# First layer of a two-layer cross-attention kernel: scores three heads ahead, values split once for all heads, two low parts on GpSimd

## Chip, cores and metric

The kernel runs on one core of one Trainium2 chip. The metric is the device time of one execution in microseconds (us). Shorter is better. The core's engines run side by side and meet only at semaphores: TensorE (PE in the rows, its weight loads PEld), VectorE (DVE), ScalarE (ACT), GpSimd (POOL), and SyncE (SP), which here only issues DMAs.

## What is computed

Two cross-attention layers, one after the other, over 4 batches of 512 queries, 512 context rows, 320 channels in 20 heads of 16. The part that the change touches is the first layer:

```
q = x @ Wq.T                      # 20 heads of 16
text = context[:77]; ip = context[77:]
out_text = softmax(q k_text.T / 4) @ v_text
out_ip   = softmax(q k_ip.T   / 4) @ v_ip      # a softmax of its own
x = (out_text + out_ip) @ Wo.T + bo + x
```

The second layer has the same sizes (508 text rows, 4 image rows, one more product) and uses another step function, which the change leaves alone.

## The kernel before

**Precision.** Products run in TensorE's rounded 32-bit format. To keep accuracy a number is split in two: a *high* part (rounded) and a *low* part (the number minus its high part), and the products of the parts are added up.

**Batch.** For each of the four batches the program does: 20 heads of layer 0, some dense products (k1, output projection, q1, the Gram matrix, v1), 20 heads of layer 1, then the inputs of layer 0 for the next batch (k0, q0, v0t, v0i) woven into the closing arithmetic of layer 1, then the output projection (tr1, y). The first three batches are turns of a loop, the fourth is written out.

**Heads of layer 0.** Every engine has a function `step0` of its own, called once per head by `run_heads` (two lead-in steps, a loop of four turns of four heads, four heads written out). In step n (head n is the one whose values are used):

- TensorE computes the scores of head n+2, queries by rows, in two halves (`scores_half`, `ps_s`), from which only the row maxima are wanted; the scores of head n+1 transposed, keys by rows, in four blocks (`scoresT_of`, `ps_t`, two buffers); the product values times probabilities of head n (`values_high`, `values_low`, `ps_w`, eight matmuls, four on high parts and four on low parts); a transpose of the maxima of head n+2 (`head_maxT`, `ps_m`); and the transposes back of the result (`ps_b`).
- ScalarE takes each transposed block twice, as exp rounded (`probsT_high`, line 454) and as exp in full (`probsT`, line 462); `shift` (line 447) copies the maxima into `q_slot`, so that the next transposed scores come out shifted; line 471 copies the head's result `ps_w` to SBUF (shown as `probs`, a buffer that is reused).
- VectorE takes the maxima (lines 638, 639), forms the low part of blocks 0, 1 and 2 (`lowT`, line 628), and adds up the result (line 653, `out_all`).
- GpSimd forms the low part of block 3 (line 376) and, for each head, copies the values of head n+2 from `v0_sb` into `v0_slot` as high parts (line 364, two CASTs) and subtracts to get the low parts (line 370, two subtractions). Both tiles are called `v_sb` and `v_slot` in the rows. These copies wait for `oT_moved`, the copy of line 471, since they overwrite the slot of the head just used.
- SyncE loads q and k parts of a head into one of four slots when the head four before it is done (`load_slots`).

The order on each engine is the order in which the code is written; nothing is reordered. `probsT` has one buffer, `probsT_high` and `probsT_low` have two each.

**Between the batches.** `v0_text` and `v0_ip` (ScalarE, lines 506 and 512) copy the value projections of the next batch from the ring of four PSUM banks into `v0_sb` and free the banks. VectorE runs a serial chain at the same time (lines 768 to 813; the last multiplications are line 805, the last addition, line 813, releases `heads_ready`). TensorE's stream there is v0t, v0i 0 to 3, then the transposes tr1 (line 1069), which wait for `heads_ready`, then y. Job i of the ring needs the bank of job i-4 to be freed.

Of the kernel before, what the change touches and what calls it, by code (L numbers as in the profile page):

```python
# [5 lines left out]
ACT = mybir.ActivationFunctionType  # L6
# [5 lines left out]
P = 128  # L12
# [33 lines left out]
V0W = 2 * (D + 1)  # L46
V0S = 2 * V0W

# [17 lines left out]
    + [("v0t", 0, "A")]  # L66
    + [("v0i", t, "A") for t in range(TB)]
# [27 lines left out]
def build(nc, xT, ctxT, mask, wq0, wk0, wv0, wki0, wvi0, wo0, bo0, wq1, wk1, wv1, wki1, wvi1, wo1, bo1, outT):  # L95
    with ExitStack() as ctx:
# [18 lines left out]
        ident = sb("ident", [P, P])  # L115
        ident_r = sb("ident_r", [P, P], F32R)
        ip_shift = sb("ip_shift", [1, T])
        ones = sb("ones", [P, 1])
        ip_rows = sb("ip_rows", [P, 1])
        v0_sb = sb("v0_sb", [P, 1 + TB, HEADS, D])  # L120
# [4 lines left out]
        ip_sq = sb("ip_sq", [P, EB, IPN])  # L125
# [16 lines left out]
        sz_all = sb("sz_all", [P, HEADS, SC, SZW])  # L142
        dump = sb("dump", [P, 16])

        heads_out = probsT[:, :, 0:C]
        heads_outT = probs[0][:, 0:CBN, :]
        outT0 = [probs[0][0:V0S, p, :] for p in range(2)]
        nd = HEADS * SC
        stat = sb("stat", [P, nd, 8])
        root = sb("root", [P, nd + IPN])  # L150
        ip_norm2 = sb("ip_norm2", [P, IPN])
        rip = sb("rip", [P, IPN])
        fused = sb("fused", [P, nd, IPN])
# [29 lines left out]
        high_in = sem("high_in")  # L183
        ip_sq_in = sem("ip_sq_in")
# [23 lines left out]
        low_last = sem("low_last")  # L208
# [3 lines left out]
        v0_high, v_high = sem("v0_high"), sem("v_high")  # L212
# [68 lines left out]
        def _(sp):  # L281
# [8 lines left out]
            for slot in k_slot:  # L290
                sp.dma_start(slot[ALL_ROWS - 1:ALL_ROWS, :].bitcast(F32), ip_shift[:, :]).then_inc(k_rows_in, 16)
# [54 lines left out]
        def _(pool):  # L346
            nc.gpsimd.memset(ident[:, :], 0.0).then_inc(filled, 1)
            nc.gpsimd.memset(ones[:, :], 1.0).then_inc(filled, 1)
            nc.gpsimd.memset(out_all[:, 0:1], 0.0).then_inc(out_moved, CREDIT)
            nc.gpsimd.memset(out_all[:, 1:2], 0.0).then_inc(low_last, CREDIT)  # L350
            pool.wait_ge(filled, 2)
            nc.gpsimd.affine_select(out=ident[:, :], in_=ident[:, :], compare_op=ALU.not_equal, fill=1.0, base=0,
                                    pattern=[[-1, P]], channel_multiplier=1).then_inc(built, 1)

            def step0(b, n, k, turn, use, transposed, scores):
                par = k % 2
                if scores:

                    pool.wait_ge(oT_moved, HEADS * b + n + 1 + CREDIT) if use else None
                    pool.sem_inc(passed, 1)  # L360
                    pieces = [(slice(0, 1), slice(0, D), v0_sb[:, 0:1, n + 2, :]),
                              (slice(0, TB), slice(D + 1, 2 * D + 1), v0_sb[:, 1:1 + TB, n + 2, :])]
                    for blocks, cols, src in pieces:
                        last = nc.gpsimd.tensor_copy(v0_slot[par][:, blocks, cols], src)  # L364
                    last.then_inc(v0_high, 1)
                    pool.wait_ge(v0_high, HEADS * b + n + 3)
                    pool.sem_inc(passed, 1)
                    for blocks, cols, src in pieces:
                        low = slice(cols.start + V0W, cols.stop + V0W)
                        last = nc.gpsimd.tensor_tensor(v0_slot[par][:, blocks, low], src, v0_slot[par][:, blocks, cols].bitcast(F32),  # L370
                                                       ALU.subtract)
                    last.then_inc(v0_in, 1)
                if transposed:

                    pool.wait_ge(pt_block[0], TB * (HEADS * b + n + 1) + TB + CREDIT1)
                    nc.gpsimd.tensor_tensor(probsT_low[1 - par][:, TB - 1, :], probsT[:, TB - 1, :],  # L376
                                            probsT_high[1 - par][:, TB - 1, :].bitcast(F32), ALU.subtract).then_inc(low_last, 1)
# [34 lines left out]
            def batch(b, ahead):  # L412
                run_heads(step0, pool, b)
# [731 lines left out]
```

## Time and profile before

| | |
|---|---|
| median of 3 runs | 1819.99 us (1816.65 to 1820.86) |
| the profiled execution's own time | 1818.08 us |
| its span, first to last instruction | 1816.3 us |
| TensorE busy | 1648.9 us, 91% |
| VectorE busy | 1279.8 us, 70% |
| ScalarE busy | 1116.6 us, 61% |
| GpSimd busy | 462.0 us, 25% |
| mean granted TensorE clock | 0.958 of 2.4 GHz |

The shares are means over stages with different limits. In the 20 heads of layer 0 ScalarE and VectorE are busiest and TensorE is not; in those of layer 1 it is the other way round. So the change has to be read from the stage that it touches.

### The profile page before, as it was taken

The numbers are of one execution on the slowest core, as the hardware profiler recorded it, in microseconds if no ns is written. First come the engines' busy times: TensorE is split into PE (matmuls) and PEld (weight loads), VectorE is DVE, ScalarE is ACT, GpSimd is POOL, SyncE is SP. The second block draws the span as 40 slices with busy tenths as digits, with TensorE's granted clock in tenths as the row PEclk, the third lists the DMA queues.
The fourth block names the chain that finished last, engine by engine and source line by source line (L and its number), as shares of the span: only waits on it lengthen the run. The fifth ranks groups of instructions, "written<-read, shape, count | busy, mean of one in ns | idle before, by whom it ended". The sixth has DMA issues, their size and how long they took to land.

```text
span 1816.3 us, 34149 instructions
## 1 busy us (share of the span) xinstructions
PE 1648.9 (91%) x8640; PEld 1240.3 (68%) x8640; DVE 1279.8 (70%) x3564; ACT 1116.6 (61%) x2323; POOL 462.0 (25%) x1225
## 2 busy tenths in 40 slices
PE   5788999999888889999988889999998889999993
PEld 2454479999445448999835545999974554799991
DVE  2587268887678627888758853888875883588875
ACT  1598157775279626777429943777734991577760
POOL 0244013232034202323104411223201440232320
PEclk9899989999989998999989998999998999899996
DMA  7210210000301031000031111100012102000000
GB/s 233 75 35 22 89 63 22 17 20 3 120 25 37 10 105 53 21 17 17 1 121 33 37 45 62 60 18 19 12 55 74 37 23 87 27 21 18 18 5 15
DMA packets 44947, 80.39 MB, mean 44 GB/s; under 512 B 4145, under 2 KB 9521, under 8 KB 44849
## 3 DMA queue, kind: packets, MB, share of 16 engines
q1 hardware_dynamic: 40736, 71.52, 11.9%
q10 hardware_dynamic: 4112, 7.73, 1.4%
q8 instruction: 40, 0.66, 0.1%
q14 instruction: 59, 0.48, 0.1%
HBM read 45.16 MB, written 34.08 MB: 44 GB/s over the span
## 4 chain that ended last, share of the span: by engine, by line
PE 78%; ACT 9%; issue 5%; DVE 5%; DMA 1%; ACTq 1%; POOL 1%; SPq 0%; POOLq 0%; DVEq 0%
PE ps_w L836 38%; PE ps_s L836 17%; PE ps_t L836 16%; PE ps_b L836 4%; ACT probsT_high L454 4%; ACT probsT L462 3%; DVE row_max L639 2%; PE ps_m L836 2%; ACT q_slot L447 1%; POOL probsT_low L376 0%; ACT probs L471 0%; ACT probs L529 0%; DMA w_ki<-in_wki 0%; PE ps_b L942 0%; DVE probs L805 0%
## 5 line engine op out<-in xcount | busy, mean ns | idle before, releaser
L454 ACT ACTIVATE probsT_high<-ps_t 128x512 fp32r<-128x512 f32 x640 | 382.6, 598 | 121.7 <-PE ps_t L836 117.4
L628 DVE TENSOR_TENSOR probsT_low<-probsT,probsT_high 128x512 fp32r<-128x512 f32 x560 | 393.1, 703 | 79.1 <-ACT probsT L462 69.8
L836 PE MATMUL ps_w<-gram,probsT_high 128*128 128x416 f32 (+2 forms) x1280 | 388.9, 315 | 0.0
L462 ACT ACTIVATE probsT<-ps_t 128x512 f32<-128x512 f32 x640 | 384.2, 600 | 0.0
L836 PE MATMUL ps_w<-gram_low,probsT_high 128*128 128x384 f32 (+2 forms) x1280 | 352.6, 304 | 0.0
L488 ACT ACTIVATE probs<-ps_s,exp_bias 128x508 f32<-128x508 f32 x320 | 220.4, 689 | 126.4 <-POOL exp_bias L387 82.4
L836 PE MATMUL ps_t<-q_slot,k_slot 98*128 98x512 f32 x640 | 267.4, 436 | 10.1 <-ACT q_slot L447 9.4
L836 PE MATMUL ps_s<-k_slot,q_slot 96*128 96x512 f32 x640 | 248.3, 432 | 27.3 <-issue 12.1
L387 POOL TENSOR_SCALAR exp_bias<-row_max 128x1 f32<-128x1 f32 x320 | 129.1, 403 | 560.5 <-DVE row_max L670 560.5
L836 PEld LDWEIGHTS ps_w<-gram_low,probsT_high 128*128 128x128 f32 (+1 forms) x1280 | 243.4, 190 | 11.0
L836 PEld LDWEIGHTS ps_w<-gram,probsT_high 128*128 128x128 f32 (+1 forms) x1280 | 242.0, 189 | 11.4
L836 PE MATMUL ps_w<-gram,probsT_low 128*128 128x400 f32 (+2 forms) x1280 | 245.4, 314 | 0.0
L670 DVE TENSOR_REDUCE row_max<-ps_s 128x1 fp32r<-128x508 f32 x320 | 216.4, 677 | 0.0
L836 PEld LDWEIGHTS ps_w<-gram,probsT_low 128*128 128x128 f32 (+1 forms) x1280 | 212.7, 190 | 0.0
L687 DVE CUSTOM_DVE_ANT_0 probs<-ps_w,probs 128x380 f32<-128x380 f32 x320 | 174.0, 544 | 0.0
L639 DVE TENSOR_REDUCE row_max<-ps_s 128x2 fp32r<-128x870 f32 x160 | 168.3, 1052 | 0.0
L836 PEld LDWEIGHTS ps_t<-q_slot,k_slot 98*128 98x128 f32 x640 | 125.0, 196 | 60.3 <-ACT probsT L462 18.6
L836 PEld LDWEIGHTS ps_s<-k_slot,q_slot 96*128 96x128 f32 x640 | 120.4, 201 | 56.6 <-issue 26.6
L376 POOL TENSOR_TENSOR probsT_low<-probsT,probsT_high 128x512 fp32r<-128x512 f32 x80 | 103.4, 1292 | 164.0 <-ACT probsT L462 164.0
L447 ACT ACTIVATE q_slot<-ps_m 2x512 fp32r<-2x512 f32 x160 | 93.6, 585 | 77.0 <-PE ps_m L836 66.1
L364 POOL CAST v_slot<-v_sb 128x16 fp32r (+3 forms) x160 | 63.7, 430 | 277.9 <-ACT probs L471 125.5
L686 DVE COPY head_out<-ps_w 128x36 f32<-128x36 f32 x320 | 62.1, 194 | 98.4 <-PE ps_w L836 98.4
(156 smaller groups left out, 2093.4 us busy)
## 6 DMA issues: line engine op xcount, KB each, us to landing
q_slot<-parts_q SPq DMA_DIRECT2D x160, 96.0 KB
k_slot<-parts_k SPq DMA_DIRECT2D x160, 96.0 KB
parts_k<-probsT_high SPq DMA_DIRECT2D x24, 512.0 KB, 4.3
parts_q<-probsT_low SPq DMA_DIRECT2D x24, 512.0 KB, 4.3
parts_k<-probsT_high SPq DMA_DIRECT2D x24, 128.0 KB, 3.8
parts_q<-probsT_low SPq DMA_DIRECT2D x24, 128.0 KB, 3.5
ctx_sb<-in_ctxT ACTq DMA_DIRECT2D x3, 1024.0 KB, 8.2
outT<-x_sb ACTq DMA_DIRECT2D x8, 256.0 KB, 4.9
```

The costliest lines, as they stand in the source:

```text
L364: last = nc.gpsimd.tensor_copy(v0_slot[par][:, blocks, cols], src)
L376: nc.gpsimd.tensor_tensor(probsT_low[1 - par][:, TB - 1, :], probsT[:, TB - 1, :], probsT_high[1 - par][:, TB - 1, :].bitcast(F32), ALU.su ...
L387: nc.gpsimd.tensor_scalar_mul(exp_bias[par][:, c:c + 1], row_max[1][par][:, c, 0:1].bitcast(F32), -SCALE)\
L447: nc.scalar.activation(q_slot[(k + 1) % SLOTS][SHIFT_ROW:ALL_ROWS, :], ps_m[0:SHIFT_ROWS, :], ACT.Copy)\
L454: nc.scalar.activation(probsT_high[1 - par][:, t, :], ps_t[:, t % 2, :], ACT.Exp, scale=SCALE)
L462: nc.scalar.activation(probsT[:, t, :], ps_t[:, t % 2, :], ACT.Exp, scale=SCALE).then_inc(pt_block[l], 1)
L488: nc.scalar.activation(probs[par][:, c, 0:TEXT1], ps_s[:, c % 2, 0:TEXT1], ACT.Exp, bias=exp_bias[par][:, c:c + 1], scale=SCALE, accum_out ...
L628: nc.vector.tensor_tensor(probsT_low[1 - par][:, t, :], probsT[:, t, :], probsT_high[1 - par][:, t, :].bitcast(F32), ALU.subtract).then_in ...
L639: nc.vector.tensor_reduce(out=row_max[0][par][:, cs, SHIFT_ROWS - 1:SHIFT_ROWS], in_=ps_s[:, :, TEXT0:T], axis=AX.X, op=ALU.max).then_inc( ...
L670: nc.vector.tensor_reduce(out=row_max[1][par][:, c, 0:1], in_=ps_s[:, c % 2, 0:TEXT1], axis=AX.X, op=ALU.max).then_inc(max_chunk, 1)
L687: nc.vector.tensor_tensor_reduce(out=probs[par][:, c, P:TEXT1], in0=ps_w[c % 2][:, 0:GN], in1=probs[par][:, c, P:TEXT1], scale=1.0, scalar ...
L836: return nc.tensor.matmul(out, lhsT, rhs, start=start, stop=stop)
```

## The change

- The scores of a head (and with them its maxima) are computed in step n for head n+3 instead of n+2. `run_heads0` has three lead-in steps instead of two. TensorE's order in a step is new: block 1 of the transposed scores, all four `values_high`, block 2, the transpose of the maxima, first half of the scores, all four `values_low`, block 3, second half of the scores, block 0 of the next head, transposes back.
- On ScalarE `shift` stands between blocks 1 and 2, and the copy of the result between blocks 2 and 3.
- Low parts: VectorE forms those of blocks 0 and 1, GpSimd those of blocks 2 and 3.
- Values are split for all 20 heads when they are projected: ScalarE writes high parts (`v0_high`, five instructions of 320 columns, as many as before), VectorE forms the low parts (`v0_lows`, five new instructions) and is now the one that frees these ring banks. Within the closing arithmetic of layer 1 `v0_lows` stands behind the last multiplications and before the last addition.
- GpSimd then only copies a head's values into `v0_slot` (128 and 32 columns), between its two low parts, and `v0_in` is what TensorE's `values_high` waits for, as before. One wait between rounding and subtracting is gone.
- Some small tiles now share memory with others; this adds no instruction to the loops.

```diff
-    + [("v0t", 0, "A")]
-    + [("v0i", t, "A") for t in range(TB)]
+    + [("v0t", 0, "D")]
+    + [("v0i", t, "D") for t in range(TB)]
...
+        def run_heads0(step, eng, b):
+            step(b, -3, 1, -1, False, False, False, True)
+            step(b, -2, 2, -1, False, False, True, True)
+            step(b, -1, 3, -1, False, True, True, True)
+            with eng.Fori(0, TURNS - 1) as turn:
+                for k in range(SLOTS):
+                    step(b, SLOTS * turn + k, k, turn, True, True, True, True)
+            for k in range(SLOTS):
+                n = HEADS - SLOTS + k
+                step(b, n, k, TURNS - 1, True, n + 1 < HEADS, n + 2 < HEADS, n + AHEAD < HEADS)
...
# GpSimd
+                def low(t):
+                    pool.wait_ge(pt_block[0], TB * (g + 1) + t + 1 + CREDIT1)
+                    pool.sem_inc(passed, 1)
+                    nc.gpsimd.tensor_tensor(probsT_low[1 - par][:, t, :], probsT[:, t, :],
+                                            probsT_high[1 - par][:, t, :].bitcast(F32), ALU.subtract).then_inc(low_pool, 1)
+                if transposed:
+                    for t in range(LOWS_DVE, TB - 1):
+                        low(t)
+                    pool.wait_ge(oT_moved, g + CREDIT)
+                    pool.sem_inc(passed, 1)
+                    by_part = v0_slot[1 - par][:, :, :].rearrange("p t (g w) -> p t g w", w=V0H)
+                    nc.gpsimd.tensor_copy(by_part[:, :, 0:2, 0:D], v0_ip[:, :, n + 1, :, :])
+                    nc.gpsimd.tensor_copy(by_part[:, 0, 2:4, 0:D], v0_text[:, n + 1, :, :]).then_inc(v0_in, 1)
+                    low(TB - 1)
...
# ScalarE
                 if transposed:
                     expT(b, 0, n, par, 0)
                     expT(b, 0, n, par, 1)
+                if shifted:
+                    shift(b, 0, n + 1, k + 1)
+                if transposed:
+                    expT(b, 0, n, par, 2)
                 if use:
                     act.wait_ge(oT_done, HEADS * b + n + 1)
                     nc.scalar.activation(outT0[par], ps_w[par][0:V0S, :], ACT.Copy).then_inc(oT_moved, 1)
-                if transposed:
-                    expT(b, 0, n, par, 2)
-                if scores:
-                    shift(b, 0, n + 1, k + 1)
                 if transposed:
                     expT(b, 0, n, par, 3)
...
# VectorE
+            def v0_lows(b):
+                before = 0 if b is FIRST else (1 + TB) * (b + 1)
+                def by_head(name, t, k):
+                    wait_job(dve, b, name, t)
+                    dve.wait_ge(v0_high_in, before + k + 1)
+                    return bank(name, t)[:, 0:C].rearrange("p (h d) -> p h d", d=D)
+                nc.vector.tensor_tensor(v0_text[0:TEXT0, :, 0, :], by_head("v0t", 0, 0)[0:TEXT0, :, :],
+                                        v0_text[0:TEXT0, :, 1, :].bitcast(F32), ALU.subtract).then_inc(freed["D"], 1)
+                for t in range(TB):
+                    nc.vector.scalar_tensor_tensor(out=v0_ip[:, t, :, 0, :], in0=by_head("v0i", t, 1 + t),
+                                                   scalar=ip_rows[:, 0:1] if t == 0 else 1.0,
+                                                   in1=v0_ip[:, t, :, 1, :].bitcast(F32),
+                                                   op0=ALU.mult, op1=ALU.subtract).then_inc(freed["D"], 1)
...
+                if shifted:
+                    maxima(g + 2, row_max[0][par], 1)
                 if transposed:
                     lowT(b, 0, n, par, 0)
                 if scores:
+                    maxima(g + AHEAD, row_max[0][1 - par], 0)
                 if transposed:
                     lowT(b, 0, n, par, 1)
                 if use:
...
-                if transposed:
-                    lowT(b, 0, n, par, 2)
...
+                    if ahead and i == 3:
+                        v0_lows(b)
                     link(b, last)
...
# TensorE
+                if transposed:
+                    scoresT_of(0, g, k, 1)
+                if use:
+                    pe.wait_ge(oT_moved, g - 1 + CREDIT)
+                    pe.wait_ge(v0_in, g + 1)
+                    for t in range(TB):
+                        values_high(t)
+                if transposed:
+                    scoresT_of(0, g, k, 2)
+                if shifted:
+                    pe.wait_ge(max_half, 2 * (g + 3) + CREDIT)
+                    head_maxT(0, par)
                 if scores:
                     scores_half(0)
                 if use:
+                    for t in range(TB - 1):
+                        values_low(t)
+                    values_low(TB - 1).then_inc(oT_done, 1)
+                if transposed:
+                    scoresT_of(0, g, k, 3)
+                if scores:
+                    scores_half(1)
+                if shifted:
+                    scoresT_of(0, g + 1, k + 1, 0)
                 if use:
                     pe.wait_ge(oT_moved, g + 1 + CREDIT)
```

## Rows read from the trace of the kernel before

**Rows 1.** Steady heads: stretch, us, busy PE PEld DVE ACT POOL, clock, DMA.
```profile
516.60:611.00 94.40, 81.47 (x411) 50.60 (x409) 84.36 (x139) 90.51 (x174) 45.56 (x87) 1.00 0.10 33
```
**Rows 2.** Timeline: result copies of heads 0, 17 and 19, second batch.
```profile
516.64 0.59 ACT L471 ACTIVATE probs<-ps_w 68x512 f32<-68x512 f32 x1
...
609.89 0.59 ACT L471 ACTIVATE probs<-ps_w 68x512 f32<-68x512 f32 x1
...
619.52 0.59 ACT L471 ACTIVATE probs<-ps_w 68x512 f32<-68x512 f32 x1 [1.91 <-PE ps_w L836]
```
**Rows 3.** Timeline of one steady head: start us, us, engine, line, operation, [idle before].
```profile
560.66 0.60 ACT L471 ACTIVATE probs<-ps_w 68x512 f32<-68x512 f32 x1
560.69 1.05 DVE L639 TENSOR_REDUCE row_max<-ps_s 128x2 fp32r<-128x870 f32 x1
...
561.52 0.92 POOL L364 CAST v_slot<-v_sb 128x16 fp32r x2 [1.89 <-ACT probs L471]
561.61 0.62 ACT L462 ACTIVATE probsT<-ps_t 128x512 f32<-128x512 f32 x1
561.66 0.68 DVE L628 TENSOR_TENSOR probsT_low<-probsT,probsT_high 128x512 fp32r<-128x512 f32 x1
...
561.79 0.40 PE L836 MATMUL ps_m<-ident_r,row_max 128*2 128x128 f32 x4 [0.45 <-DVE row_max L639]
...
562.04 0.41 PE L942 MATMUL ps_b<-ident,probs 68*128 68x68 f32 x4
...
562.25 0.58 ACT L447 ACTIVATE q_slot<-ps_m 2x512 fp32r<-2x512 f32 x1
562.25 0.71 PE L836 MATMUL ps_s<-k_slot,q_slot 96*128 96x512 f32 x2
...
562.80 0.87 PE L836 MATMUL ps_w<-probsT_high,v_slot 128*68 128x512 f32 x3
562.86 0.60 ACT L454 ACTIVATE probsT_high<-ps_t 128x512 fp32r<-128x512 f32 x1
...
563.35 0.59 ACT L462 ACTIVATE probsT<-ps_t 128x512 f32<-128x512 f32 x1
...
563.57 0.30 DVE L638 TENSOR_REDUCE row_max<-ps_s 128x2 fp32r<-128x154 f32 x1
563.80 1.05 DVE L639 TENSOR_REDUCE row_max<-ps_s 128x2 fp32r<-128x870 f32 x1
...
564.02 1.30 POOL L376 TENSOR_TENSOR probsT_low<-probsT,probsT_high 128x512 fp32r<-128x512 f32 x1 [0.92 <-ACT probsT L462]
...
565.06 0.81 DVE L628 TENSOR_TENSOR probsT_low<-probsT,probsT_high 128x512 fp32r<-128x512 f32 x1 [0.21 <-ACT probsT L462]
```
**Rows 4.** GpSimd by shape, all stretches: count | busy us, mean ns | idle before.
```profile
L376 POOL TENSOR_TENSOR probsT_low<-probsT,probsT_high 128x512 fp32r<-128x512 f32 x80 | 103.4, 1292 | 164.0 <-ACT probsT L462 164.0
L364 POOL CAST v_slot<-v_sb 128x64 fp32r x64 | 49.3, 771 | 0.0
...
L364 POOL CAST v_slot<-v_sb 128x64 fp32r<-128x64 f32 x16 | 3.8, 240 | 0.0
...
L418 POOL CAST gram<-gram 128x128 fp32r<-128x128 f32 x4 | 1.2, 293 | 0.0
```
**Rows 5.** Timeline of the lead-in of layer 0, second batch.
```profile
500.55 1.21 PE L836 MATMUL ps_s<-k_slot,q_slot 96*128 96x512 f32 x2 [5.01 <-issue]
...
507.92 0.60 ACT L454 ACTIVATE probsT_high<-ps_t 128x512 fp32r<-128x512 f32 x1 [0.96 <-PE ps_t L836]
```
**Rows 6.** Timeline between batches one and two.
```profile
482.21 2.32 PE L836 MATMUL ps_s<-w_vi,ctx_sb 128*128 128x320 f32 x8
482.38 1.49 DVE L813 TENSOR_TENSOR probsT<-probs 128x1280 f32<-128x1280 f32 x1
...
484.36 0.60 PE L1069 MATMUL ps_s<-ident,probsT 128*128 128x128 f32 x4
484.56 0.44 ACT L512 ACTIVATE v_sb<-ps_s 128x320 f32<-128x320 f32 x1 [1.72 <-PE ps_s L836]
```

More of the change, by code:

```diff
@@ L563, in batch @@
                     highs(b, "q0")
-                    v0_text(b)
-                    for t in range(TB):
-                        v0_ip(b, t)
+                    v0_high(b)
                 move_transposed(b, "tr1")
@@ L573, in _ @@
             highs(FIRST, "q0")
-            v0_text(FIRST)
-            for t in range(TB):
-                v0_ip(FIRST, t)
+            v0_high(FIRST)
             run_batches(act, batch)
@@ L605, in _ @@
             for slot in v0_slot:
-                last = nc.vector.memset(slot[0:TEXT0, 0, 2 * D + 1:V0W].bitcast(F32), 0.0)
+                last = nc.vector.memset(slot[0:TEXT0, 0, V0W - 1:V0W].bitcast(F32), 0.0)
             last.then_inc(dve_consts_in, 1)
@@ L629, in lowT, with step0, maxima @@
                                         ALU.subtract).then_inc(low_block[l], 1)
-            def step0(b, n, k, turn, use, transposed, scores):
+            def step0(b, n, k, turn, use, transposed, shifted, scores):
                 par = k % 2
-                def maxima(half):
+                g = HEADS * b + n
+                def maxima(j, rows, half):
                     cs = slice(2 * half, 2 * half + 2)
-                    dve.wait_ge(s_half, 2 * (HEADS * b + n + 2) + half + 1)
-                    nc.vector.tensor_reduce(out=row_max[0][par][:, cs, 0:1], in_=ps_s[:, :, 0:TEXT0], axis=AX.X, op=ALU.max)
-                    nc.vector.tensor_reduce(out=row_max[0][par][:, cs, SHIFT_ROWS - 1:SHIFT_ROWS], in_=ps_s[:, :, TEXT0:T],
+                    dve.wait_ge(s_half, 2 * j + half + 1)
+                    nc.vector.tensor_reduce(out=rows[:, cs, 0:1], in_=ps_s[:, :, 0:TEXT0], axis=AX.X, op=ALU.max)
+                    nc.vector.tensor_reduce(out=rows[:, cs, SHIFT_ROWS - 1:SHIFT_ROWS], in_=ps_s[:, :, TEXT0:T],
                                             axis=AX.X, op=ALU.max).then_inc(max_half, 1)
-                if scores:
-                    maxima(0)
+                if shifted:
+                    maxima(g + 2, row_max[0][par], 1)
                 if transposed:
@@ L824, in _ @@
             lows(FIRST, "q0")
+            v0_lows(FIRST)
             run_batches(dve, batch)
@@ L883, in head_maxT, with step0 @@
                 last.then_inc(maxT_done[l], 1)
-            def step0(b, n, k, turn, use, transposed, scores):
+            def step0(b, n, k, turn, use, transposed, shifted, scores):
                 par = k % 2
```

150 lines of the change are left out of this document (58 added, 92 removed).

## The prediction

> **What bounds the kernel now.** I read four views: the table of stretches, to see how full each engine is in the 20 heads of layer 0; the timeline of one steady head, for durations, distances between starts and what ends each wait; GpSimd's rows by shape; and the timeline around the hand-over from batch to batch.
>
> In the steady heads of a batch ScalarE is busy 90.51 of 94.40 us, VectorE 84.36, TensorE 81.47, GpSimd 45.56, at full TensorE clock (2.4 GHz) [rows 1]. Head 0's result copy starts at 516.64 and head 17's at 609.89: 93.25 us for 17 heads, a period P of 5.485 us; the last two heads take 9.63 us together [rows 2]. In each period TensorE sits 0.45 us until VectorE's second maxima are done (561.74), and only then come the transposed maxima, the copy into q_slot at 562.25 and the next scores, on which VectorE's next maxima hang [rows 3]. So the period is a loop between VectorE and TensorE, with ScalarE just behind. The other layer and the dense products are untouched; layer 0 is 4 x 20 heads, and 0.1 us of P is worth 4 x 17 x 0.1 = 6.8 us.
>
> **What the change takes away.** Scores three heads ahead give the maxima nearly a whole head of room, and VectorE loses one subtraction of 0.68 us per head. Its loop goes. ScalarE's ten instructions remain. Their starts lie 0.48 to 0.49 apart (562.86 to 563.35), but a copy into q_slot begins only when the exp before it has ended (561.61 + 0.62 = 562.23, start 562.25) and the next exp 0.61 after it (562.86) [rows 3]. Eight distances of 0.48, one of 0.62 and one of 0.61 make 5.07 us: the floor that is left.
>
> **What it adds: a loop through GpSimd.** TensorE's new step runs all four high products before block 2 of the transposed scores and before the transposed maxima, and the high products wait for v0_in. GpSimd gives v0_in for a head only after the low part of block 2 of that head, because the copies stand behind it in its program. The copy into q_slot (start s), which ScalarE does between blocks 1 and 2, waits for the transposed maxima. That closes a loop of one head. From rows:
>
> - s to the first exp of block 2: 0.61; to the second: 0.49; its length 0.59 [rows 3]. Together 1.69.
> - ScalarE's end to GpSimd's start: the copies start at 561.52 after an end at 561.26, 0.26; the subtraction, with no semaphore step between wait and instruction, at 564.02 after 563.94, 0.08 [rows 3]. The new `low` has that step: 0.27.
> - The subtraction of 128x512 on GpSimd: 1.29 [rows 4].
> - The two copies. 128 columns were not timed in this pattern; the nearest are CASTs of 128 columns at 293 ns and of 64 at 240 ns [rows 4]. The small one adds some 0.14. I take 0.43, bounds 0.35 and 0.9 (two of 64 with a slot pattern, and once more as long).
> - GpSimd to TensorE: 0.05, as from VectorE (561.74 to 561.79) [rows 3].
> - Four high products and block 2: three matmuls take 0.87, the last one's run-out counted in, so 0.24 to 0.29 each [rows 3]; I take 0.24: 5 x 0.24 = 1.20. Transposed maxima 0.40, to ScalarE 0.06 (562.19 to 562.25) [rows 3].
>
> Sum: 1.69 + 0.27 + 1.29 + 0.43 + 0.05 + 1.20 + 0.40 + 0.06 = 5.39 us, if nothing holds GpSimd up.
>
> Something does. Where GpSimd's 64-column CAST meets VectorE's subtraction with two SBUF inputs it takes 771 ns, and 240 where VectorE does none [rows 4]. In the timeline the CASTs start at 561.52, the subtraction at 561.66 ends at 562.34, and the CASTs end at 562.44 [rows 3]: GpSimd stood until VectorE was through, and needed only 0.10 more instead of 0.24, so 0.14 of an instruction can be spent while standing. The other way, VectorE's subtraction at 565.06 takes 0.81 beside GpSimd's that ends at 565.32 [rows 3].
>
> Now the new order. Transposed maxima start at s - 0.46, the first half of the scores 0.25 behind (562.04 after 561.79) and takes 0.71: done at s + 0.50. VectorE's maxima start at s + 0.54, the second reduction 0.23 later, and the subtraction of block 1 another 0.97 later (560.69 to 561.66) [rows 3]: s + 1.74 to s + 2.43. GpSimd's subtraction of block 2 is ready at s + 1.96, in the middle of it. It loses 0.47 less 0.14, some 0.3 us, every head. P = 5.39 + 0.30 = 5.69, slower than now.
>
> The Trainium skill, page "SBUF — State Buffer", section "Who interferes with whom", says that a VectorE instruction with two SBUF inputs and a GpSimd instruction that reads SBUF exclude each other, whichever starts first holding the interface for its whole length. By that rule the trace agrees (771 against 240 ns), the collision above goes to VectorE and P is 5.69; with the order of the two starts turned round it would be 5.39.
>
> **The lead-in.** Before, block 0 of the first transposed scores is in ScalarE's hands at 507.92, 7.4 us after the first scores at 500.55 [rows 5]. Now a half of another head's scores, at half clock (two matmuls 1.21 us), and its maxima (0.23 + 1.05) come before it: +2.4. Then the first high products wait for block 2, subtraction and copies on GpSimd, where before three of them ran on blocks already there: +0.9. I take +3.3 per batch, bounds 2.4 and 4.5.
>
> **The end.** The last two steps have no scores; with result copies late in ScalarE's order little follows them. Head 17's lies at s + 1.57. Head 18's: v0_in at s + 3.73, five matmuls and the run-out of the last 1.36, two exps 1.01: s + 6.1, 4.5 later. Head 19's: exp 0.11, wait 0.27, two subtractions 2.58, copies 0.43, last low product 0.45: 3.9 later. 8.4 against 9.63 [rows 2]: -1.2. The turns of the inner loop keep their small extra, some 0.05 us per head in the mean.
>
> Per batch: 3.3 - 1.2 + 17 x (P + 0.05 - 5.485). With P = 5.69 this is 2.1 + 4.3 = +6.4; four batches, +25.6.
>
> **The hand-over.** VectorE's last addition started at 482.38 and TensorE's tr1 at 484.36, right behind v0i 3 (482.21 + 2.32) [rows 6]. Now v0_lows stands before that addition. The bank of v0i 3 is that of v0t, freed only by the first of the lows, about 482.35 + 0.45 = 482.8. So v0i 3 ends at 485.2, its high part (0.44) at 485.7, its low part (0.5, between ScalarE's 0.44 and VectorE's 0.68 for 512 columns) at 486.2, the addition (1.49) at 487.7, tr1 at 488.0: +3.6 us, on TensorE's path. Three such hand-overs: +10.8. Bounds: 2.5 (the addition held up for five lows alone) and 4.5. In the first batch the lows end while TensorE still waits for its slots; nothing there, and at most 1. ScalarE's high parts write as many columns as before: nothing.
>
> Slots: a head's load now has one head less to arrive, still over 7 us from request to use; two issues and one landing fit in. If not, it is in the worst case below.
>
> Sum: 25.6 + 10.8 = +36.4, on the profiled execution's own 1818.08 us, which lies 0.1% under the median of the runs: 1854 us.
>
> **Rivals.**
>
> A, the collision is missed. If VectorE's subtraction of block 1 starts 0.25 us later than I laid it out, GpSimd holds the interface and VectorE waits, which it can afford. P = 5.39: 2.1 + 17 x (-0.045) = +1.3 per batch, 5 + 11 = +16: 1834. For it: only 0.22 us separate the two starts. Against: both hang on the same s by short steps.
>
> B, faster than before. GpSimd's leg from exp to v0_in (0.27 + 1.29 + 0.43 + 0.05 = 2.04 us) does not set the period, because the high products and the maxima come through sooner than I chain them; then ScalarE's 5.07 rules: 2.1 - 6.2 = -4.1 per batch, -16 + 11: 1812; 1801 if the hand-over is hidden too. It decides from P = 5.15 down (68 x (5.44 - P) = 8.4 + 10.8), so the leg would have to be under about 1.8 us. For it: ScalarE's wait for the maxima really goes. Against: the 1.29 is measured 80 times and the copies stand behind it in the program. Between A and B lies no change: P near 5.15, 1815 to 1822.
>
> C, worse than forecast. The copies meet a subtraction too, or take 0.9, or VectorE's block 0, held up by GpSimd's block 3, pushes the maxima: P near 5.95, 2.1 + 8.7 = +10.8 per batch, 43 + 11: 1872.
>
> D, the change does not do what it says, if the copies were still casts plus subtractions, cannot be: they are gone from the code.
>
> **How the numbers follow.** Forecast (1843 to 1862) 0.47, A (1824 to 1843) 0.21, C (over 1862) 0.12, no change 0.06, B 0.14. 1854 is the forecast's value. For 8 in 10 the range leaves out B's faster part and C's far end: 1814 to 1870. A measurement of this kernel tells 0.2% (3.6 us) from no change. Faster 0.14, same 0.06, slower 0.80.
>
> **What would show it.** In the changed trace: result copies of layer 0 5.6 to 5.7 us apart; TensorE's high products waiting for GpSimd's copies, ScalarE waiting some 0.6 us a head before the copy into q_slot; GpSimd's block 2 about 1.6 us long in the mean and block 3 about 1.3; VectorE with over a microsecond idle per head; tr1 some 3.6 us later after the last multiplications; the first result copy 19 us after the first scores instead of 16.1. Wrong if the copies into q_slot follow the exps at once (B), if block 2 takes 1.3 (A), or if tr1 keeps its place.

## The result: 1863 us, 2.5% slower than before

| | before | after |
|---|---|---|
| median of the runs | 1818.32 us (1815.70 to 1820.86, 4 runs) | 1863.28 us (1859.68 to 1869.03, 4 runs) |
| profiled execution: time, span | 1818.08, 1816.3 us | 1859.68, 1857.9 us |
| mean granted TensorE clock | 0.958 | 0.955 |

The ratio of the times is 1.025, 95% interval 1.0224 to 1.0276: slower, 45 us where 36 were forecast. The profiled executions lie 41.6 us apart.

The table of stretches of the changed kernel, the answer to [rows 1]. Columns: stretch in us, its length, busy us of PE, PEld, DVE, ACT and POOL with instructions, granted clock, DMA share, GB/s. First 17 steady heads of batch two, then its lead-in, then y's products after the hand-over.

```profile
536.10:634.90 98.80, 84.67 (x407) 52.31 (x406) 74.26 (x119) 85.98 (x171) 56.20 (x68) 1.00 0.09 30
515.20:536.10 20.90, 15.06 (x42) 8.38 (x42) 11.53 (x17) 8.87 (x17) 3.36 (x4) 0.54 0.03 11
499.50:507.60 8.10, 8.02 (x13) 2.65 (x13) 0.75 (x1) 0.00 (x0) 0.00 (x0) 0.73 0.24 90
```

ScalarE and VectorE are less full than before (87% and 75%, against 96% and 89%), at the same full clock, and the heads take longer: no engine's total is the bound, so a chain of waits is.

The timeline of the changed kernel: result copies of heads 0 and 17, the answer to [rows 2].

```profile
536.15 0.59 ACT L495 ACTIVATE probs<-ps_w 68x512 f32<-68x512 f32 x1
...
634.91 0.59 ACT L495 ACTIVATE probs<-ps_w 68x512 f32<-68x512 f32 x1
```

17 heads in 98.76 us: P = 5.81 us, against 5.485. The last two take 9.50 us together. One steady head of it, the answer to [rows 3] (start us, us, engine, line, operation, idle before and its releaser):

```profile
563.73 0.59 ACT L467 ACTIVATE q_slot<-ps_m 2x512 fp32r<-2x512 f32 x1 [0.72 <-PE ps_m L867]
...
564.84 0.59 ACT L482 ACTIVATE probsT<-ps_t 128x512 f32<-128x512 f32 x1
...
565.46 0.68 DVE L657 TENSOR_TENSOR probsT_low<-probsT,probsT_high 128x512 fp32r<-128x512 f32 x1
...
565.60 1.67 POOL L385 TENSOR_TENSOR probsT_low<-probsT,probsT_high 128x512 fp32r<-128x512 f32 x1 [2.51 <-ACT probsT L482]
...
567.22 0.29 POOL L395 CAST v_slot<-v_ip 128x128 fp32r x1
...
567.45 0.21 POOL L396 CAST v_slot<-v_text 128x32 fp32r x1
...
567.62 1.29 POOL L385 TENSOR_TENSOR probsT_low<-probsT,probsT_high 128x512 fp32r<-128x512 f32 x1
...
567.90 1.14 PE L867 MATMUL ps_w<-probsT_high,v_slot 128*68 128x512 f32 x4 [0.47 <-ACT probsT L482]
...
569.12 0.40 PE L867 MATMUL ps_m<-ident_r,row_max 128*2 128x128 f32 x4
...
569.56 0.59 ACT L467 ACTIVATE q_slot<-ps_m 2x512 fp32r<-2x512 f32 x1 [0.74 <-PE ps_m L867]
```

From one copy into q_slot to the next, 5.83 us: that copy and the two exps of block 2 to their end (563.73 to 565.43) 1.70; to GpSimd 0.17; subtraction 1.67; two copies 0.39; to TensorE 0.24; high products and block 2 (567.90 to 569.12) 1.22; transposed maxima 0.40; to ScalarE 0.04. The row of the profile names ScalarE's exp as the releaser of the high products. An exp (567.22 + 0.62) did end 0.06 before they start, GpSimd's last copy 0.24 before. But by ScalarE's order of work that exp is block 0's of the next head, and `values_high` waits only for the four blocks of its own head, which were done at 566.87. That leaves GpSimd's copy; experiments 1 and 2 test it.

GpSimd by shape over the whole program, the answer to [rows 4] (count | busy us, mean ns | idle before):

```profile
L385 POOL TENSOR_TENSOR probsT_low<-probsT,probsT_high 128x512 fp32r<-128x512 f32 x160 | 230.6, 1441 | 450.8 <-ACT probsT L482 450.7
L395 POOL CAST v_slot<-v_ip 128x128 fp32r x64 | 19.5, 305 | 0.0
```

The lead-in of batch two, the answer to [rows 5]: first scores, first exp, VectorE's subtraction beside GpSimd's, first copy for TensorE, first high products.

```profile
515.19 1.21 PE L867 MATMUL ps_s<-k_slot,q_slot 96*128 96x512 f32 x2 [4.67 <-issue]
...
525.00 0.60 ACT L474 ACTIVATE probsT_high<-ps_t 128x512 fp32r<-128x512 f32 x1 [3.40 <-PE ps_t L867]
...
529.56 1.61 DVE L657 TENSOR_TENSOR probsT_low<-probsT,probsT_high 128x512 fp32r<-128x512 f32 x1
...
530.56 0.76 POOL L395 CAST v_slot<-v_ip 128x128 fp32r<-128x128 f32 x1
...
531.71 1.97 PE L867 MATMUL ps_w<-probsT_high,v_slot 128*68 128x512 f32 x4
```

The hand-over from batch one to two, the answer to [rows 6]:

```profile
489.33 1.70 DVE L833 TENSOR_TENSOR probs<-out_all,vip_rep 128x320 f32<-128x320 f32 x4
490.95 0.48 DVE L646 TENSOR_TENSOR v_text<-ps_s,v_text 77x320 fp32r<-77x320 f32 x1
...
491.48 2.42 PE L867 MATMUL ps_s<-w_vi,ctx_sb 128*128 128x320 f32 x8 [0.42 <-DVE v_text L646]
...
494.41 0.49 DVE L649 SCALAR_TENSOR_TENSOR v_ip<-ps_s,v_ip 128x320 fp32r<-128x320 f32 x1 [1.73 <-ACT v_ip L531]
...
494.82 1.48 DVE L843 TENSOR_TENSOR probsT<-probs 128x1280 f32<-128x1280 f32 x1
...
496.54 0.63 PE L1096 MATMUL ps_s<-ident_r,probsT 128*128 128x128 f32 x4 [2.63 <-DVE probsT L843]
```

**Where the 41.6 us came from**, by the same waypoints in both profiled executions:

| stretch | before, batches 1 to 4 | after | sum | forecast |
|---|---|---|---|---|
| first scores to first result copy | 16.52, 16.09, 16.77, 15.98 | 20.55, 20.96, 21.39, 20.64 | +18.2 | +13.2 |
| head 0's result copy to head 19's | 102.94, 102.88, 102.89, 102.40 | 107.17, 108.26, 106.89, 105.43 | +16.6 | +12.4 |
| last multiplications to tr1 | 3.72 three times | 7.21 three times | +10.5 | +10.8 |
| tr1 to the next first scores | 16.19, 15.80, 12.34 | 18.65, 15.82, 13.56 | +3.7 | 0 |
| last projection of the program | 10.32 | 6.00 | -4.3 | 0 |
| all the rest | | | -3.1 | 0 |

The row of -4.3 is no work of the change: the same 12 matmuls, first in the kernel before, then in the changed one.

```profile
1799.53 10.32 PE L836 MATMUL ps_s<-probs,w_o 128*128 128x512 f32 x12 [0.68 <-ACT probs L529]
```
```profile
1845.48 6.00 PE L867 MATMUL ps_s<-probs,w_o 128*128 128x512 f32 x12 [0.68 <-ACT probs L547]
```

They differ in the granted clock (0.67 in 1796 to 1816 of before). Without it the profiled executions would lie 45.9 us apart; the medians lie 45 apart. What makes up the row of -3.1 was not followed up.

### The profile page after: what moved, and what is told of

The parts are those of the page before. It is cut to its first block, busy times and chain, and to the rows that moved or that the text cites. A ratio compares the mean times of both kernels' runs of the same rounds, so it can differ in the third digit from the quotient of the medians.

```text
span 1857.9 us, 33840 instructions
## 1 busy us (share of the span) xinstructions
PE 1669.9 (90%) x8640; PEld 1253.8 (67%) x8640; DVE 1249.7 (67%) x3504; ACT 1102.8 (59%) x2323; POOL 513.8 (28%) x1145
## 4 chain that ended last, share of the span: by engine, by line
PE 72%; ACT 13%; issue 7%; DVE 6%; DMA 1%; ACTq 1%; SPq 0%; POOL 0%; DVEq 0%; POOLq 0%
PE ps_w L867 37%; PE ps_t L867 14%; PE ps_s L867 14%; ACT probsT_high L474 6%; PE ps_b L867 4%; ACT probsT L482 4%; PE ps_m L867 2%; DVE probs L833 1%; DVE probs L842 1%; ACT probs L495 1%; DVE row_max L669 1%; DMA w_ki<-in_wki 0%; ACT q_slot L467 0%; DVE row_max L698 0%; ACT probs L547 0%
## 5 line engine op out<-in xcount | busy, mean ns | idle before, releaser
L657 DVE TENSOR_TENSOR probsT_low<-probsT,probsT_high 128x512 fp32r<-128x512 f32 x480 | 353.4, 737 | 48.1 <-ACT probsT L482 41.9
L385 POOL TENSOR_TENSOR probsT_low<-probsT,probsT_high 128x512 fp32r<-128x512 f32 x160 | 230.6, 1441 | 450.8 <-ACT probsT L482 450.7
L867 PE MATMUL ps_t<-q_slot,k_slot 98*128 98x512 f32 x640 | 281.5, 443 | 26.2 <-ACT q_slot L467 10.4
L867 PE MATMUL ps_s<-k_slot,q_slot 96*128 96x512 f32 x640 | 253.8, 441 | 47.3 <-DVE row_max L669 29.3
L867 PEld LDWEIGHTS ps_s<-k_slot,q_slot 96*128 96x128 f32 x640 | 115.5, 203 | 98.8 <-DVE row_max L669 66.9
L867 PE MATMUL ps_w<-probsT_high,v_slot 128*68 128x512 f32 x320 | 94.9, 420 | 31.3 <-ACT probsT L482 23.7
```

The source lines that it names most:

```text
L385: nc.gpsimd.tensor_tensor(probsT_low[1 - par][:, t, :], probsT[:, t, :], probsT_high[1 - par][:, t, :].bitcast(F32), ALU.subtract).then_in ...
L657: nc.vector.tensor_tensor(probsT_low[1 - par][:, t, :], probsT[:, t, :], probsT_high[1 - par][:, t, :].bitcast(F32), ALU.subtract).then_in ...
L867: return nc.tensor.matmul(out, lhsT, rhs, start=start, stop=stop)
```

## The experiments

All start from the changed kernel but for experiment 9, which starts from the kernel before. Ratios are to the kernel before, timed in the same rounds.

### 1. GpSimd copies the values before block 2's subtraction

```diff
 # GpSimd, step0
-                    for t in range(LOWS_DVE, TB - 1):
-                        low(t)
                     pool.wait_ge(oT_moved, g + CREDIT)
...
                     nc.gpsimd.tensor_copy(by_part[:, 0, 2:4, 0:D], v0_text[:, n + 1, :, :]).then_inc(v0_in, 1)
+                    for t in range(LOWS_DVE, TB - 1):
+                        low(t)
                     low(TB - 1)
```

> The changed kernel with one edit: in each step GpSimd makes the two copies of the values before the low part of block 2 instead of behind it. Theory G (GpSimd's leg, exp of block 2, subtraction, copies, v0_in, sets the period of 5.82 us): the copies leave the loop, TensorE's high products start once the exp of block 3 is there, the copy into q_slot follows ScalarE's exps at about 5.1 us per head; 68 x 0.7 = 48 us less than the changed kernel, about 1815 us. Rival S (the high products wait for ScalarE's exp, as the releaser named in the trace says, and the new order on TensorE and ScalarE sets the period): 5.8 us per head, about 1863 us.

Measured: 1835.39 us, ratio 1.0089 (1.0066 to 1.0112). The timeline of this kernel:

```profile
561.08 0.68 PE L866 MATMUL ps_s<-k_slot,q_slot 96*128 96x512 f32 x2
...
563.14 0.73 PE L866 MATMUL ps_s<-k_slot,q_slot 96*128 96x512 f32 x2 [0.22 <-DVE row_max L668]
...
563.94 0.41 PE L968 MATMUL ps_b<-ident_r,probs 68*128 68x68 f32 x4
...
564.49 0.44 DVE L682 TENSOR_REDUCE out_all<-ps_b 128x272 f32 x1 [0.81 <-PE ps_b L968]
...
564.80 1.10 PE L866 MATMUL ps_w<-probsT_high,v_slot 128*68 128x512 f32 x4
565.02 0.32 DVE L667 TENSOR_REDUCE row_max<-ps_s 128x2 fp32r<-128x154 f32 x1
...
566.36 0.40 PE L866 MATMUL ps_m<-ident_r,row_max 128*2 128x128 f32 x4 [0.23 <-DVE row_max L668]
```

The high products (564.80) no longer wait, and 28 us of the 45 are gone. The exps are the same, so they were not what released the products: GpSimd's leg was. But the period came down to 5.34 in three heads of four and 5.52 in the fourth, not to the 5.1 of ScalarE's floor. The row at 566.36 says what is late now: VectorE's second maxima, which in its program stand behind the sum of the result (564.49), which waits 0.81 for the transposes back, which stand behind the second half of the scores (563.14) and block 0, which wait for VectorE's first maxima. A second loop, under the first one by only 0.3 to 0.5 us, that my prediction had not seen. Experiment 5 tests it.

### 2. Block 1's subtraction on VectorE before the first maxima

```diff
 # VectorE, step0
                 if transposed:
                     lowT(b, 0, n, par, 0)
-                if scores:
-                    maxima(g + AHEAD, row_max[0][1 - par], 0)
                 if transposed:
                     lowT(b, 0, n, par, 1)
+                if scores:
+                    maxima(g + AHEAD, row_max[0][1 - par], 0)
```

> The changed kernel with one edit: VectorE forms the low part of block 1 before its first maxima instead of behind them, so that it is over before GpSimd starts on block 2. Theory G with the collision as its second part: GpSimd's subtraction of block 2 falls from 1.66 to 1.29 us, the period from 5.82 to 5.44; 68 x 0.38 = 26 us less, about 1837 us. Rival S, or the collision off the path: 5.8 us per head, 1860 us or more.

Measured: 1840.41 us, 1.0109 (1.0083 to 1.0134), period 5.45. Its rows of GpSimd by shape, and the same step in its timeline:

```profile
L385 POOL TENSOR_TENSOR probsT_low<-probsT,probsT_high 128x512 fp32r<-128x512 f32 x160 | 205.2, 1283 | 460.5 <-ACT probsT L482 460.5
```
```profile
560.50 1.29 POOL L385 TENSOR_TENSOR probsT_low<-probsT,probsT_high 128x512 fp32r<-128x512 f32 x1 [2.53 <-ACT probsT L482]
...
561.96 0.21 POOL L396 CAST v_slot<-v_text 128x32 fp32r x1
...
562.41 1.14 PE L867 MATMUL ps_w<-probsT_high,v_slot 128*68 128x512 f32 x4
```

GpSimd does the same work in the same order; only VectorE's instruction was moved out of its way, and the subtraction takes 1.29 instead of 1.67 us. The period falls by 0.37, the collision's whole price. And 0.24 us lie again between GpSimd's last copy (ends 562.17) and the high products (562.41), which now start before the exp that the page had named is over (562.11 + 0.62 = 562.73 here).

### 3. Three low parts on VectorE again, the third at the end of its step

```diff
-LOWS_DVE = 2
+LOWS_DVE = 3
...
 # VectorE, step0, behind the sum of the result
+                if transposed:
+                    lowT(b, 0, n, par, 2)
```

> The changed kernel with one part undone: VectorE forms the low parts of blocks 0, 1 and 2 again (block 2 at the end of its step), GpSimd only that of block 3. Theory G: the copies no longer wait for a subtraction, VectorE has room for 0.62 us more, so the period falls to 5.1 to 5.2 us: 1816 to 1822 us. Rival S: 5.8 us per head, about 1863 us. If VectorE became the bound it would be 5.4 to 5.5: 1837 us.

Measured: 1937.73 us, 1.0637 (1.0605 to 1.0669), period 6.85. The worst miss of the series.

```profile
560.58 0.44 DVE L683 TENSOR_REDUCE out_all<-ps_b 128x272 f32 x1 [0.81 <-PE ps_b L971]
...
560.67 1.29 POOL L385 TENSOR_TENSOR probsT_low<-probsT,probsT_high 128x512 fp32r<-128x512 f32 x1 [4.70 <-ACT probsT L482]
...
560.93 1.58 DVE L657 TENSOR_TENSOR probsT_low<-probsT,probsT_high 128x512 fp32r<-128x512 f32 x1
...
563.77 0.40 PE L869 MATMUL ps_m<-ident_r,row_max 128*2 128x128 f32 x4 [1.56 <-DVE row_max L669]
```

GpSimd had less to do, and by the ratios the kernel was 70 us slower than the changed one. The third subtraction went into experiment 1's second loop, between the sum and the second maxima, and there it met GpSimd's own subtraction: this time GpSimd had started first and VectorE stood, 1.58 us for a 0.68 us instruction. From the start of the sum to that of the second maxima it is 1.86 us here (560.58 to 562.44) and 0.36 in experiment 1's heads of 5.34 us; 5.34 + 1.50 = 6.84, the period seen. I had counted what VectorE does and not where in its program the instruction stands.

### 4. The values' low parts spread around the last addition

```diff
-            def v0_lows(b):
+            def v0_lows(b, blocks=range(-1, TB)):
...
+                    if ahead and i == 2:
+                        v0_lows(b, (-1,))
                     if ahead and i == 3:
-                        v0_lows(b)
+                        v0_lows(b, (0,))
...
                 nc.vector.tensor_tensor(by_head, w4[0], w4[1], ALU.add).then_inc(heads_ready, 1)
+                if ahead:
+                    v0_lows(b, (1, 2, 3))
```

> The changed kernel with one edit: the five low parts of the values are spread over VectorE's closing chain (text before the last multiplications, block 0 behind them, blocks 1 to 3 behind the last addition). Theory: the bank of the fourth value block is free in time and the last addition waits for one low part instead of five; the transposes of the heads follow the last multiplications by about 4.5 us instead of 7.2; 3 x 2.7 = 8 us less, and up to 7 more where TensorE's clock fell in the first hand-over: 1848 to 1856 us. Rival (the hand-over is covered by other work): 1861 to 1865 us.

Measured: 1850.01 us, 1.0172 (1.0147 to 1.0196), 14 us less than the changed kernel by the ratios. Its hand-over:

```profile
491.54 0.63 PE L1101 MATMUL ps_s<-ident_r,probsT 128*128 128x128 f32 x4 [0.18 <-DVE probsT L846]
...
493.89 6.00 PE L872 MATMUL ps_s<-probs,w_o 128*128 128x512 f32 x12 [0.85 <-ACT probs L547]
```

TensorE's idle before tr1 is 0.18 instead of 2.63 us, and y's twelve matmuls take 6.00 us where the changed kernel's took 8.09 (its row stands with point 4 below). The 10.5 and the 3.7 us of the table went together: in this trace tr1 follows the last multiplications by 3.79 us, and the next first scores follow tr1 by 16.01, 16.22 and 12.37.

### 5 and 6. Both loops opened, with two or three low parts on VectorE

Experiment 5 is experiment 1 with this on VectorE:

```diff
-                if shifted:
-                    maxima(g + 2, row_max[0][par], 1)
                 if transposed:
                     lowT(b, 0, n, par, 0)
...
                 if transposed:
                     lowT(b, 0, n, par, 1)
+                if scores:
+                    maxima(g + AHEAD, row_max[0][1 - par], 1)
                 if use:
                     dve.wait_ge(o_done, g + 1)
```

> e1 (copies ahead of block 2 on GpSimd) with a second edit: VectorE takes the second-half maxima of head g+3 at the end of its own step, before the sum of the result, instead of behind that sum at the start of the next step. Theory L (with GpSimd off the path, e1 is held at 5.35 to 5.5 us by a loop first maxima, second half of the scores, transposes back, sum of the result, second maxima, transposed maxima, whose steps add to 5.36 us): the sum leaves the loop and ScalarE's own chain of 5.07 us is left; 5.1 to 5.15 us per head, 20 us less than e1, about 1815 us. Rival (ScalarE is held by something else, its floor is higher than worked out): 5.35 us, about 1835 us.

Experiment 6 is experiment 3 with the second maxima moved in the same way and `lowT(b, 0, n, par, 2)` between block 1's and them, before the sum.

> e3 (VectorE forms three low parts, GpSimd one) with VectorE's order changed: low 0, first maxima, low 1, low 2, second maxima of the same head, sum of the result. Theory L: e3's 6.85 us came from where the third low part stood (behind the sum and before the second maxima, and against GpSimd's subtraction), not from how much VectorE has to do (4.6 us): 5.1 to 5.2 us per head, 1812 to 1822 us. Rival (VectorE is full with three low parts three heads ahead): above 5.4, 1835 us or more.

Measured: 1814.60 us, 0.9974 (0.9960 to 0.9988), and 1811.51 us, 0.9972 (0.9958 to 0.9986); period 5.13 in both. In experiment 5 the second maxima start before the sum of the result, and the copy into q_slot follows ScalarE's exp with no wait:

```profile
556.45 0.32 DVE L667 TENSOR_REDUCE row_max<-ps_s 128x2 fp32r<-128x154 f32 x1 [0.23 <-PE ps_s L866]
...
557.65 0.43 DVE L682 TENSOR_REDUCE out_all<-ps_b 128x272 f32 x1
...
558.96 0.58 ACT L466 ACTIVATE q_slot<-ps_m 2x512 fp32r<-2x512 f32 x1
```

That is the second loop shown by its removal. Experiment 6 holds the same instructions as experiment 3 in another order on VectorE, and is some 120 us faster by the ratios; between experiments 5 and 6 the ratios show no difference.

### 7 and 8. Experiments 5 and 6 with the other two costs mended

Both with experiment 4's hand-over and this in TensorE's lead-in:

```diff
+                if shifted and not transposed:
+                    scoresT_of(0, g + 1, k + 1, 0)
                 if scores:
                     scores_half(1)
-                if shifted:
+                if shifted and transposed:
                     scoresT_of(0, g + 1, k + 1, 0)
```

> e5 with the spread low parts of the values of e4, and in the lead-in the first transposed scores of head 0 ahead of the second half of head 1's scores. If the three costs add up: 1815 less 13 for the hand-overs less 4 x 1 to 2 for the lead-in, about 1797 us, 1.2% under the kernel before. If they don't (ScalarE or TensorE takes back what one frees): 1805 to 1815 us.

> e6 with the same two edits as e7. By the same sum about 1797 us; if GpSimd's subtractions no longer meet VectorE's, up to 5 us under e7, otherwise up to 10 over it.

Measured: 1796.80 us, 0.9889 (0.9861 to 0.9917), with two low parts on GpSimd; 1793.77 us, 0.9871 (0.9851 to 0.9892), with one. The second has the lowest median of the series, 1.3% under the kernel before (1817.72 in the same rounds); the intervals of the two overlap, so which of them is faster is not shown. Its steady stretch, and two copies into q_slot:

```profile
514.50:606.00 91.50, 84.76 (x423) 54.39 (x422) 81.63 (x140) 90.04 (x180) 39.53 (x54) 1.00 0.10 33
```
```profile
553.90 0.58 ACT L467 ACTIVATE q_slot<-ps_m 2x512 fp32r<-2x512 f32 x1
...
559.01 0.58 ACT L467 ACTIVATE q_slot<-ps_m 2x512 fp32r<-2x512 f32 x1
```

ScalarE is busy 90.04 of 91.50 us: now an engine is the bound. The copies are 5.11 apart and wait for nothing.

### 9. The split of the values alone, in the kernel before

Scores two heads ahead, the old order and three low parts on VectorE; only the values are split once for all heads, with experiment 4's spread, and GpSimd's four casts and subtractions per head become two copies.

```diff
 # GpSimd, step0 of the kernel before: casts and subtractions out, in their place
+                    nc.gpsimd.tensor_copy(by_part[:, :, 0:2, 0:D], v0_ip[:, :, n + 2, :, :])
+                    nc.gpsimd.tensor_copy(by_part[:, 0, 2:4, 0:D], v0_text[:, n + 2, :, :]).then_inc(v0_in, 1)
```

> The kernel before (scores two heads ahead, three low parts on VectorE, all step orders as before) with one part of the change: values split once for all heads, with the low parts spread over VectorE's closing chain as in e4, and GpSimd only copying. Theory: in the kernel before the period of 5.45 us is VectorE's and TensorE's loop, in which GpSimd's copies have no place, so it stays 5.45; the hand-over costs 3 x 1 us: 1818 to 1822 us, no gain. Then what e7 and e8 gain over the kernel before comes from the scores three heads ahead. Rival: the split alone is worth something (fewer meetings of GpSimd and VectorE), 5.3 us per head, about 1808 us.

Measured: 1813.95 us, 0.9983 (0.9972 to 0.9993). A small gain, some 4 us below the time expected; the steady period is that of before, and GpSimd's small copy still meets a subtraction of VectorE:

```profile
555.29 0.67 POOL L384 CAST v_slot<-v_text 128x32 fp32r x1
555.32 0.40 PE L864 MATMUL ps_m<-ident_r,row_max 128*2 128x128 f32 x4 [0.67 <-DVE row_max L660]
```

TensorE waits for the second maxima as in [rows 3]. So taking work from GpSimd gives next to nothing here; most of experiment 8's 24 us came with the third head ahead and the order.

### 10. Only the lead-in's order

The lead-in edit of experiments 7 and 8 on the changed kernel alone.

> The changed kernel with one edit in the lead-in: the first transposed scores of head 0 ahead of the second half of head 1's scores. The lead-in was 4.0 to 4.9 us longer than before, of which 2.5 are scores and maxima ahead of the first exp; the edit gives back at most that and rather 1 to 2 us of each of four: 1855 to 1860 us against 1863. Rival (the lead-in is set by the scores and maxima of head 2, which are as late as before): 1863 us.

Measured: 1857.40 us, 1.0221 (1.0201 to 1.0240). Its lead-ins last 19.72, 20.30, 20.34 and 20.01 us, 0.6 to 1.1 less than the changed kernel's. In batch two the first exp (522.69) comes 7.37 us after the first scores (515.32), as it did before the change, and yet the first high products come only 0.85 us earlier than in the changed kernel:

```profile
522.69 0.60 ACT L474 ACTIVATE probsT_high<-ps_t 128x512 fp32r<-128x512 f32 x1 [0.96 <-PE ps_t L867]
...
530.99 1.97 PE L867 MATMUL ps_w<-probsT_high,v_slot 128*68 128x512 f32 x4
```

The rest of the 2.4 us is lost to the next wait: block 2 and its subtraction on GpSimd stand behind the maxima of the extra head.

## Why the prediction was right, and where its sizes were off

**1. The bound was named rightly.** After the change no engine limits layer 0 but a loop of one head: exps, GpSimd's subtraction, its copies, the high products, the transposed maxima. Experiment 1 cut it by moving two copies and gained 28 us; experiment 2 took only the collision out of it (the same steps add up to 5.45 us in its trace) and gained 0.37 us per head, 23 us in the total. Of the marks I had set, the high products do follow GpSimd's copies, ScalarE waits 0.72 to 0.74 us before the copy into q_slot (0.6 forecast), block 2 takes 1.67 (1.6) and block 3 1.29 (1.3), VectorE is idle 24.5 us in 17 heads, 1.4 per head (over 1). The result copies are 5.81 apart, above the 5.6 to 5.7.

**2. P came out at 5.83 where the sum said 5.69.** Term by term, forecast and measured: exps 1.69 and 1.70; to GpSimd 0.27 and 0.17; subtraction with collision 1.59 and 1.67; copies 0.43 and 0.39; to TensorE 0.05 and 0.24; products and block 2 1.20 and 1.22; maxima and last step 0.46 and 0.44. The wait and the collision were each off and make up for each other: GpSimd started 0.10 earlier and so stood 0.08 longer, for it went on only when VectorE was through (565.46 + 0.68 = 566.14). The term that failed is GpSimd to TensorE, for which I took the 0.05 that lies between VectorE and TensorE. It is 0.24 in the steady heads of batches one to three, in the changed kernel and in experiment 2 alike. I had given "GpSimd to TensorE" one value and no bounds although no row of before showed this pair; that was against my own way of costing the rest.

The 0.24 is no fixed price of the pair, though. In batch four, which is written out behind the loop over the batches, the same wait takes about 0.10 us in three steady heads of four, and so it does in the last three heads of every batch:

```profile
1486.87 0.20 POOL L396 CAST v_slot<-v_text 128x32 fp32r x1
...
1487.18 1.11 PE L867 MATMUL ps_w<-probsT_high,v_slot 128*68 128x512 f32 x4 [0.33 <-issue]
```

Where it is short, the result copies of batch four lie 5.63 to 5.67 us apart; in every fourth head it is 0.25 again, and they lie 5.82 apart. So some 0.14 us of the term hang on where in the program TensorE's wait stands; by what mechanism no run shows. In the mean of all 68 steady heads the period is 5.76 us, against 5.69 and the 0.05 that I had added for the turns of the loop: the missed 0.19 came in full in three batches only, and the turns' extra, which I had expected in all four, only in the fourth. The closeness of 5.76 and 5.74 is in part luck. The steady heads took 19.1 us more than before where 17.3 were forecast.

The other half of the miss in the heads (+16.6 against +12.4) is the term of -1.2 per batch for the last two heads. In batches one and three they took 8.54 and 8.53 us, 1.1 less than before, as forecast; in batches two and four 9.50 and 9.43, hardly less than before. The granted clock in these stretches was 1.00 in the first pair and 0.82 in the second; before the change it was 1.00 in all four. Together -2.5 us instead of -4.8.

**3. The lead-in was under-costed, 4.6 us per batch instead of 3.3.** The first part held: first exp 9.81 us after the first scores instead of 7.37, +2.44 for +2.4. The second, from the first exp to the first result copy, grew from 8.72 to 11.15, +2.43 where I had +0.9, though my bounds for the whole reached 4.5; three of the four lead-ins lie above them (4.0, 4.9, 4.6 and 4.7). The granted clock is 0.54 there, as low as in the lead-in before the change (0.56), so the four high products take 1.97 us instead of 1.14, and GpSimd's copy met VectorE's subtraction, which itself stood behind GpSimd's (1.61 and 0.76 us in the rows above). I had priced this part from rows at full clock.

**4. The hand-over held: 3.49 us each for a forecast of 3.6.** The order of events was the one written down, v0i 3 behind the text's low part, the last addition behind the last low part. Not foreseen was what came behind it. After an idle of 2.63 us y's matmuls ran at a lower granted clock, 0.73:

```profile
499.58 8.09 PE L867 MATMUL ps_s<-probs,w_o 128*128 128x512 f32 x12 [0.76 <-ACT probs L547]
```

The three stretches cost 3.7 us more than before; with experiment 4's order, without the idle, the twelve take 6.00 in all three. The other traces bear the link out. Seven kernels have the idle of 2.63 us before tr1 (the changed one and experiments 1, 2, 3, 5, 6 and 10), 21 hand-overs: in 15 of them TensorE was slowed between tr1 and the end of y's twelve matmuls. Five have 0.18 or none (the kernel before and experiments 4, 7, 8 and 9), 15 hand-overs: in all of them tr1 and the twelve matmuls kept their times of before. So the idle lets the clock fall, but does not always: after batch two of the changed kernel the same idle stands and the stretch took 15.82 us against 15.80. What decides it in one hand-over is open. Experiments 5 and 6 still pay for this (their profiled executions lost clock in three and one of three hand-overs), so part of what 7 and 8 gain over them is the clock.

**5. The rivals.** A, a missed collision, had P 5.39: the collision was there, and experiment 2 shows what the kernel would have been without it, 5.45 and 1840. B needed GpSimd's leg under 1.8 us; it is 0.17 + 1.67 + 0.39 + 0.24 = 2.47. B's floor is real: with the leg off the path the period is 5.13, 0.06 above the 5.07 worked out from ScalarE's ten distances, and the total 1815 as B's 1812 would have it. The result lies halfway between the forecast and C (P 5.95, 1872), but not by C's mechanisms: the 128-column copy takes 305 ns in the mean and does not collide in the steady heads, and VectorE's subtraction of block 0, which GpSimd's of block 3 does hold up (0.97 us instead of 0.68, from 568.50), pushes nothing, for VectorE then waits 0.61 us for scores. The median of 1863.28 lies just over the 1862 at which the forecast's own bracket (chance 0.47) ends, in the one that I had given to C (0.12). What I had not listed is the second loop of experiment 1, at 5.34 and more: it would have kept B's case from coming true even with GpSimd's leg short, as experiment 1 itself shows with 1.0089. That the total came so near owes something to terms that I had at nothing and that partly cancel: +3.7 for the clock, -4.3 for one slow stretch of the kernel before, -3.1 for the rest.

**6. The interface shared by VectorE and GpSimd.** The traces show it both ways: GpSimd's subtraction 1.67 beside VectorE's and 1.28 alone, VectorE's 1.58 behind GpSimd's and 0.68 alone. By the rule that the prediction drew from the Trainium skill, page "SBUF — State Buffer", section "Who interferes with whom", that whichever of the two starts first holds the other up, the traces agree in both directions. So the engines do not meet only at semaphores: this shared interface is a second place, and in experiment 3 it held VectorE up by 0.9 us a head.

## What to carry to other kernels

Moving work to an idle engine is paid by the place it takes in that engine's program: ask which short instruction stands behind it and who waits for that one, as here two copies of 0.2 to 0.3 us behind a subtraction of 1.3. The same instructions on VectorE in two orders differed by some 120 us (experiments 3 and 6), more than any count of work had in it. And when one loop is opened, work out the next one before hoping for the floor: three loops here lay between 5.1 and 5.8 us.

## What the runs showed of the hardware that I had not expected

- From the end of GpSimd's copy to the TensorE instruction waiting for it 0.24 us in one place of the program (567.66 to 567.90, 562.17 to 562.41) and 0.11 in another (1487.07 to 1487.18); from VectorE to TensorE 0.05.
- A releaser printed beside a wait can be a coincidence: ScalarE's exp was named for the high products, which by the code do not wait for that exp, and in experiment 2 they start before it ends.
- The same twelve matmuls took 6.00, 8.09 and 10.32 us in different places and executions, at granted clocks of 1.00, 0.73 and 0.57. Behind an idle of 2.63 us the clock fell in 15 hand-overs of 21, without it in none of 15.
- An instruction of 0.2 us that stands while VectorE's runs takes its length: GpSimd's 128x32 copy 0.67 instead of 0.21, its 128x128 copy 0.76 instead of 0.29.
